# Merged attention in one stage: products of probabilities and values in 32 bit from one copy, exponentials run ahead, VectorE steps reordered

## The reference

```
# branch "b": quantized causal self attention in each block of 128 tokens
q, k, v = bitlinear(x, Wq), bitlinear(x, Wk), bitlinear(x, Wv)   # rope on q, k
p = softmax(causal(q k^T / sqrt(32)));  out = bitlinear(p v, Wo)
x = layernorm(x + out)
# branch "c": gated cross attention to 128 memory tokens
q = rmsnorm(x) wq^T;  k, v = memory wk^T, memory wv^T
p = softmax(masked(q k^T / sqrt(32)));  out = sigmoid(x wg^T) * (p v wo^T)
x = layernorm(x + out)
```

## Time and profile before

| | us |
|---|---|
| time, median of 3 runs | 3196.19 (3192.08 to 3197.03) |
| the profiled execution's own time | 3198.22 |
| span from the first to the last instruction in it | 3196.4 |
| PE busy in the span | 2819.0 (88%) |
| VectorE (DVE) busy | 1944.5 (61%) |
| ScalarE (ACT) busy | 1589.0 (50%) |

### The profile page before, as it was taken

The page is one execution under the profiler, slowest core; times in us unless marked ns, Lnnn a source line. Parts: engine busy times, 40 slices in busy tenths (PEclk is TensorE's granted clock), DMA queues, the critical chain, the costliest instruction groups (busy, mean ns, idle before and its releaser), DMA issues. The chain is left out here.

```text
span 3196.4 us, 50865 instructions
## 1 busy us (share of the span) xinstructions
PE 2819.0 (88%) x17698; PEld 1620.0 (51%) x17698; DVE 1944.5 (61%) x3635; ACT 1589.0 (50%) x3632; POOL 1205.6 (38%) x1234
## 2 busy tenths in 40 slices
PE   6889877999999999699669888887669999999998
PEld 4676653555555555244236555554434444444443
DVE  5788978778788787676567777764442212222224
ACT  7999955655555564643167666654421222122211
POOL 4888967645455452243231111110312221222211
PEclk8999998999999999899879999999779999999999
DMA  4111113000000000400210000000000000000001
GB/s 154 54 42 41 47 51 105 14 8 7 4 7 7 4 3 1 158 1 1 78 41 18 15 13 16 15 15 14 33 31 31 31 31 1 31 31 31 1 1 53
DMA packets 35090, 99.06 MB, mean 31 GB/s; under 512 B 4933, under 2 KB 9413, under 8 KB 31686
## 3 DMA queue, kind: packets, MB, share of 16 engines
q1 hardware_dynamic: 34886, 96.46, 9.1%
HBM read 87.79 MB, written 4.46 MB: 29 GB/s over the span
## 5 line engine op out<-in xcount | busy, mean ns | idle before, releaser
L945 DVE TENSOR_TENSOR m_prod<-m_bank,m_gated 128x512 f32<-128x512 f32 x96 | 66.4, 692 | 507.3 <-ACT m_gated L776 507.3
L720 POOL TENSOR_TENSOR m_aTl<-m_prod,m_aTh 128x512 bf16<-128x512 f32 x96 | 110.9, 1155 | 675.0 <-ACT m_aTh L778 675.0
L1926 POOL TENSOR_TENSOR s_state<-s_state,s_ct 128x512 f32<-128x512 f32 x256 | 326.8, 1307 | 83.1 <-DVE s_state L2101 81.1
L2101 DVE TENSOR_TENSOR_SCAN s_state<-s_decay,s_psd 128x512 f32<-128x512 f32 x256 | 301.9, 1209 | 67.7 <-PE s_psd L2246 34.1
L776 ACT ACTIVATE m_gated<-m_bank 128x512 f32<-128x512 f32 x96 | 57.2, 596 | 549.8 <-PE m_bank L1037 549.8
L1035 PE MATMUL m_bank<-m_xTh,m_wh 128*128 128x512 bf16 x768 | 292.5, 381 | 0.0
L1037 PE MATMUL m_bank<-m_xTh,m_wl 128*128 128x512 bf16 x768 | 292.5, 381 | 0.0
L1036 PE MATMUL m_bank<-m_xTl,m_wh 128*128 128x512 bf16 x768 | 292.5, 381 | 0.0
L2246 PE MATMUL s_psd<-ident,s_v 128*128 128x128 f32 x1024 | 164.7, 286 | 42.4 <-DVE s_state L2101 21.9
L2002 ACT ACTIVATE s_decay<-s_dt,s_nega 128x508 f32<-128x508 f32 x256 | 181.8, 711 | 19.5 <-DVE s_state L2101 19.4
L2015 ACT ACTIVATE s_v<-s_uT,s_bT 128x512 f32<-128x512 f32 x256 | 182.4, 714 | 1.1 <-PE s_psd L2246 1.0
(11 more groups left out here) (499 smaller groups left out, 8142.7 us busy)
## 6 DMA issues: line engine op xcount, KB each, us to landing
m_stage<-in_moe_w_dram SPq DMA_DIRECT2D x8, 2352.0 KB, 9.5
s_ct<-ssm_bc SPq DMA_DIRECT2D x64, 256.0 KB, 3.1
X<-in_x_dram SPq DMA_DIRECT2D x4, 1024.0 KB, 11.6
a_cf<-in_ctxT_dram SPq DMA_DIRECT2D x16, 256.0 KB, 2.6
a_wstage<-in_xa_wq_dram SPq DMA_DIRECT2D x8, 512.0 KB, 3.6
a_wstage<-in_xa_wo_dram SPq DMA_DIRECT2D x8, 512.0 KB, 3.9
f_wstage<-in_ffn_wg_dram SPq DMA_DIRECT2D x4, 1024.0 KB, 6.2
f_wstage<-in_ffn_wu_dram SPq DMA_DIRECT2D x4, 1024.0 KB, 5.2
```

Source lines behind the costliest of these rows:

```text
L1926: pool.tensor_tensor(h, h, ct[t % 4][:, s * P:(s + 1) * P].unsqueeze(1).broadcast_to([P, KB, P]), ALU.mult).then_inc(weighted, 1)
L2101: dve.tensor_tensor_scan(state[i % RING][:, :], decay[t % 2][:, s, :, :].rearrange("p m t -> p (m t)"), ps_d[i % 2][:, :], 0.0, ALU.mult, ...
```

## The change

- The bf16 pairs `pTh`/`pTl` and `vh`/`vl` go. One 32-bit tile `pT` (ScalarE's copy of `ps_t`) and one 32-bit tile `v` take their place, and one 32-bit matmul per head takes the place of three bf16 ones. VectorE's `low_part` (8 in a merged turn) and the rests of both values (one each per turn) go. Where something waited for `low`, it waits for ScalarE's copy (`copied`).
- In sequences that an attention handles alone (`single`: 0 to 3 for `core`, 12 to 15 for `mcore`), odd groups write their probabilities to the other attention's `prob` tile, which is idle there, and ScalarE issues the exponentials of group g+1 ahead of the copy of group g.
- The steps on VectorE and a few on ScalarE stand in another order: steps that release a bank of PE come before layer-norm statistics and divisions.

The core of the diff (the other parts rename semaphores, and remove `values` and `memory_values` from VectorE, with ScalarE's copies writing the 32-bit `v` tiles):

```diff
-        self.vh = [sb(f"{tag}_vh{j}", [P, key_groups * P], BF16, st) for j in range(2)]
-        self.vl = [sb(f"{tag}_vl{j}", [P, key_groups * P], BF16, st) for j in range(2)]
+        self.v = [sb(f"{tag}_v{j}", [P, key_groups * P], F32, st) for j in range(2)]
...
-        self.pTh = sb(f"{tag}_pTh", [P, 4, P], BF16, st)
-        self.pTl = sb(f"{tag}_pTl", [P, 4, P], BF16, st)
+        self.pT = sb(f"{tag}_pT", [P, 4, P], F32, st)
...
+    def alone(self, s):
+
+        return isinstance(s, int) and s in self.single
+
+    def prob_of(self, s, g):
+
+        return self.second if self.alone(s) and g % 2 else self.prob
+
     def turn_probs(self, pe, s, g, other, turned_by_other):
         pe.wait_ge(self.exps.sem, self.exps.at(s, g + 1))
         if g or late(s, 1):
-            pe.wait_ge(self.low.sem, self.low.at(s, g) if g else self.low.at(s - 1))
+            pe.wait_ge(self.copied.sem, self.copied.at(s, g) if g else self.copied.at(s - 1))
         if not isinstance(turned_by_other, int) or turned_by_other:
-            pe.wait_ge(other.low.sem, turned_by_other)
+            pe.wait_ge(other.copied.sem, turned_by_other)
         for h in range(4):
-            mm = pe.transpose(self.ps_t[:, h * P:(h + 1) * P], self.prob[:, h, :], self.fr.ident[:, :])
+            mm = pe.transpose(self.ps_t[:, h * P:(h + 1) * P], self.prob_of(s, g)[:, h, :], self.fr.ident[:, :])
         mm.then_inc(self.turned.sem, 1)
...
             v = (4 * g + h if self.KG == 4 else h) * self.HW
             out = self.ps_v[:, (4 * g + h) * self.HW:(4 * g + h + 1) * self.HW]
-            mm = three(pe, out, (self.pTh[:, h, :], self.pTl[:, h, :]),
-                       (self.vh[p][:, v:v + self.HW], self.vl[p][:, v:v + self.HW]), True, True)
+            mm = pe.matmul(out, self.pT[:, h, :], self.v[p][:, v:v + self.HW], start=True, stop=True)
         mm.then_inc(self.pv.sem, 1)
...
     def exponentials(self, act, s, g, p):
         act.wait_ge(self.shifted.sem, self.shifted.at(s, g + 1))
-        if g or late(s, 1):
+        if self.alone(s):
+            if g >= 2:
+                act.wait_ge(self.turned.sem, self.turned.at(s, g - 1))
+            elif s >= 1:
+                act.wait_ge(self.turned.sem, self.turned.at(s - 1, 3 if g == 0 and self.alone(s - 1) else 4))
+        elif g or late(s, 1):
             act.wait_ge(self.turned.sem, self.turned.at(s, g) if g else self.turned.at(s - 1))
         if g == 0 and late(s, 2):
             act.wait_ge(self.recip.sem, self.recip.at(s - 2))
         for h in range(4):
-            e = act.activation(self.prob[:, h, :], self.ps_s[:, h * P:(h + 1) * P], ACT.Exp,
+            e = act.activation(self.prob_of(s, g)[:, h, :], self.ps_s[:, h * P:(h + 1) * P], ACT.Exp,
                                bias=self.shift[g % 2][:, h:h + 1], scale=self.SCALE,
                                accum_out=self.total[p][:, 4 * g + h:4 * g + h + 1])
         e.then_inc(self.exps.sem, 1)
 
-    def high_part(self, act, s, g):
+    def copy_part(self, act, s, g):
         act.wait_ge(self.turned.sem, self.turned.at(s, g + 1))
         if g or late(s, 1):
             act.wait_ge(self.pv.sem, self.pv.at(s, g) if g else self.pv.at(s - 1))
-        act.activation(self.pTh[:, :, :].rearrange("p h t -> p (h t)"), self.ps_t[:, :], ACT.Copy).then_inc(self.high.sem, 1)
+        act.activation(self.pT[:, :, :].rearrange("p h t -> p (h t)"), self.ps_t[:, :], ACT.Copy).then_inc(self.copied.sem, 1)
...
-    def low_part(self, dve, s, g):
-        dve.wait_ge(self.high.sem, self.high.at(s, g + 1))
-        dve.tensor_tensor(self.pTl[:, :, :].rearrange("p h t -> p (h t)"), self.ps_t[:, :],
-                          self.pTh[:, :, :].rearrange("p h t -> p (h t)"), ALU.subtract).then_inc(self.low.sem, 1)
...
-        core = PairCore(fr, st, "b", 1, PairCore.HW ** -0.5, ps_t, 1)
+        core = PairCore(fr, st, "b", 1, PairCore.HW ** -0.5, ps_t, 1, range(0, LAG))
...
-        mcore = PairCore(fr, st, "c", 4, 1.0, ps_t, 64)
+        mcore = PairCore(fr, st, "c", 4, 1.0, ps_t, 64, range(SEQS - LAG, SEQS))
+        core.second, mcore.second = mcore.prob, core.prob
...
+                    has_b = live(s) and (g < 3 or live(s + 1)) or g == 3 and live(s + 1)
+                    has_c = live(m) and (g < 3 or live(m + 1)) or g == 3 and live(m + 1)
+                    if has_b and core.alone(s):
+                        core.exponentials(act, *following(s, g, p))
...
                     if live(s):
-                        core.high_part(act, s, g)
-                    if live(s) and (g < 3 or live(s + 1)) or g == 3 and live(s + 1):
+                        core.copy_part(act, s, g)
+                    if has_b and not core.alone(s):
                         core.exponentials(act, *following(s, g, p))
+                    if has_c and mcore.alone(m):
+                        mcore.exponentials(act, *following(m, g, p))
                     if g == 0:
                         if live(s + 2):
...
                     if g == 2:
-                        if live(m + 1):
-                            memory_values(m + 1, o)
...
                     if live(m):
-                        mcore.high_part(act, m, g)
-                    if live(m) and (g < 3 or live(m + 1)) or g == 3 and live(m + 1):
+                        mcore.copy_part(act, m, g)
+                    if has_c and not mcore.alone(m):
                         mcore.exponentials(act, *following(m, g, p))
                     if g == 0 and live(m + 1):
                         high(nTh[o][:, :], bank[1][:, :], n_turned, m + 1, n_high)
                     if g == 1 and live(s + 2):
                         qx.scalar(act, s + 2)
-                    if g == 2 and live(m + 2):
-                        context_high(m + 2, p)
+                    if g == 2:
+                        if live(m + 1):
+                            memory_values(m + 1, o)
+                        if live(m + 2):
+                            context_high(m + 2, p)
...
                     if g == 2:
                         if live(s - 1):
                             qo.clip(dve, s - 1)
-                        if live(s - 2):
-                            ln.statistics(dve, s - 2)
                         if live(s + 1):
                             query_low(s + 1, o)
                             key_low(s + 1, o)
                     if g == 3 and live(s - 2):
                         ln.vector_end(dve, s - 2)
-                    if live(s):
-                        core.low_part(dve, s, g)
                     if g == 0:
                         if live(s + 1):
                             rotate_keys(s + 1, o)
-                            values(s + 1, o)
-                        if live(s - 1):
-                            core.divide(dve, s - 1, o)
+                    if g == 2 and live(s - 2):
+                        ln.statistics(dve, s - 2)
                     if g == 3 and live(s + 3):
                         quantize_x(s + 3, o)
 
                     if live(m) and (g < 3 or live(m + 1)) or g == 3 and live(m + 1):
                         mcore.maxima(dve, *following(m, g, p)[:2])
-                    if g == 0 and live(m - 1):
-                        mcore.divide(dve, m - 1, o)
-                    if g == 1:
-                        if live(m - 1):
-                            low(oTl[:, :], bank[1][:, :], oTh[:, :], o_high, m - 1, o_low)
-                        if live(m - 2):
-                            mln.vector_end(dve, m - 2)
+                    if g == 1 and live(m - 1):
+                        low(oTl[:, :], bank[1][:, :], oTh[:, :], o_high, m - 1, o_low)
                     if g == 3:
                         if live(m + 2):
                             norm_mean(m + 2)
                         if live(m - 1):
                             gate_output(m - 1, o)
-                    if live(m):
-                        mcore.low_part(dve, m, g)
-                    if g == 0 and live(m + 1):
-                        low(nTl[o][:, :], bank[1][:, :], nTh[o][:, :], n_high, m + 1, n_low)
-                    if g == 1 and live(m + 1):
-                        queries_low(m + 1, o)
-                    if g == 2 and live(m + 1):
-                        memory_values(m + 1, o)
-                    if g == 3:
-                        if live(m + 2):
-                            norm_apply(m + 2)
+                            memory_end(m - 1)
+                    if g == 0:
+                        if live(s - 1):
+                            core.divide(dve, s - 1, o)
                         if live(m - 1):
-                            memory_end(m - 1)
+                            mcore.divide(dve, m - 1, o)
+                        if live(m + 1):
+                            low(nTl[o][:, :], bank[1][:, :], nTh[o][:, :], n_high, m + 1, n_low)
+                    if g == 1:
+                        if live(m + 1):
+                            queries_low(m + 1, o)
```

(24 more changed lines are left out.)

2 lines of the change are left out of this document (1 added, 1 removed).

## The result

The changed kernel takes 3142.80 us (median of 4 runs, 3140.32 to 3148.05) against 3196.61 us of the kernel before on the same chip: a ratio of 0.9833, 95% interval 0.982 to 0.9845. That is 1.7% faster; 1.2% was predicted (3157 us). The profiled execution took 3140.32 us.

What follows compares the result with a forecast made beforehand. PE nearly sets the pace in merged turns (84% busy), a chain of waits in turns 0 to 2 and 16 to 18. Terms -14 - 1 + 3 - 2 + 0 - 20 - 5 = -39 us gave 3157 us, range 3130 to 3184.

Steps and rivals of the forecast that it cites:

- The 32-bit product: On PE, every group of values: four products take 0.97 us, 0.65 us more than before; 46.8 us over nine merged turns.
- groups of values of about 0.97 us: Sign expected in the changed profile: PE's groups of values take about 0.97 us, against 0.31 us before.
- All four waits should go, 1 us stays: Merged turns: PE's waits for c_pTl, b_ln_r, b_kd, c_qTl (49.6 of 53.7 us) go; 1 us a turn stays for quantized x.
- Nearly the whole gain of the removed waits is given back: Nine merged turns: the 32-bit product's PE time takes back nearly all the removed waits, 335.7 us against 338.1, -2 us.
- Turns 16 to 18: Second attention alone: 22.3 us of waits for exponentials go, PE sets the pace, products add 7.8 us; 78 us, -20.
- Turns 0 to 2: First attention alone: the chain stays but shortens to 21 us a turn, 63 us against 77.4, -14.
- the keys of group 3: Turns 0 to 2: group 3 takes longer, its scores needing new keys and queries that ScalarE splits after the exponentials.
- Half the idle time staying: Rival, merged turns: ScalarE takes VectorE's place and 27 us of PE's idle time stays; 3175 us, chance 0.15.
- Run-ahead worth half: Rival, one-attention turns: VectorE's and ScalarE's other steps are next late, half of 39 us is lost; 3177 us, chance 0.12.
- The dear product: Rival, PE in every group: each product takes four loads, 1.94 us a group; slower, 3262 us, chance 0.08.
- The cheap product: Rival, PE in every group: the product's cost goes with its columns, 0.5 us a group; 3132 us, chance 0.12.
- The wait in front of the transposes of `c_o`: Turns 16 to 18: a new small PE wait, as these transposes need c_nTl from the same bank; 0.9 us a turn.

Runs made afterwards that it cites:

- run with 64 columns: The changed kernel with three of a group's four 32-bit products multiplying 64 columns of the values instead of 32: 3145.21 us, ratio 0.9849.
- run with the early quantization: The changed kernel with ScalarE quantizing x in group 1 ahead of the second attention's copy and exponentials, instead of behind them: 3134.74 us, ratio 0.9809.
- first-attention-only run: The changed kernel with the exponentials' run-ahead kept in the first attention and taken out of the second: 3181.42 us.
- mixed kernel: The changed kernel with bf16 pairs, low parts and rests back in merged turns 4 to 15, 32-bit products kept in one-attention turns: 3126.37 us, ratio 0.9789.

## Why the prediction came out as it did

| stretch | predicted us | measured us |
|---|---|---|
| turns 0 to 2, from the first exponentials | -14 | -10.0 |
| turn 3 | -1 | -0.9 |
| turns 4 and 5 | +3 | -0.1 |
| nine merged turns | -2 | -14.9 |
| turn 15 | 0 | -2.5 |
| turns 16 to 18 | -20 | -23.8 |
| turn 19 | -5 | -3.7 |

The measured column adds up to -55.9 us against -39. In the two profiles the first exponentials also come 3.3 us earlier in the changed kernel, and what follows the last turn takes 1.3 us longer, both in stages that the change doesn't touch. That makes the 57.9 us between the two spans; the medians are 53.8 us apart.

The signs that the prediction named for the changed profile are there: merged turns of 35.9 us (it said 37.3) with PE busy for 97%, turns 16 to 18 of 24.8 us (26), turns 0 to 2 of 21.8 us (21), and 512 pieces for each attention.

*The 32-bit product.* The one clearly mis-sized term. I took 8 x 0.121 = 0.97 us; it is 0.81. The 0.97 was misread: it is the duration that the router's row shows for its eight weight loads, not the time until the next step. The changed kernel shows the same duration for its own eight loads, beside a pace of 0.81 us, and the router's next step starts 0.91 us (2295.50 - 2294.59) after its first piece:

```profile
1907.31 0.97 PEld L2454 LDWEIGHTS b_psv<-b_v,b_pT 128*128 128x128 f32 x8
```
```profile
2295.50 0.66 PE L986 MATMUL m_bank<-ident,m_xs 128*128 128x128 f32 x4
```

So "groups of values of about 0.97 us" came true to the letter (0.98 is shown) while the price is lower. From start to start the router's row gives 0.114 us a piece; why it is 0.10 here is open. Over the 72 groups that is 11.5 of the 12.9 us that the merged turns came out shorter, and over the 24 groups of turns 4, 5 and 15 3.8 of 5.6. The mechanism (two pieces a product, a price that the columns don't set) was right, and the run with 64 columns shows it.

*All four waits should go, 1 us stays.* Right: the four rows are gone, and the one left is 0.9 us a turn, for `b_q_int`, as named. The run with the early quantization shows that it was a real loss.

*"Nearly the whole gain of the removed waits is given back."* Right in sign, too strong. By the runs the order alone takes 28.8 us off the nine turns; the 32-bit product then gives 13.8 back (31.2 us more busy, 17.4 less idle). So half is kept. What I had not seen: the order alone removes half of the idle time (53.7 to 25.6 us) without touching a product. The wait for `b_ln_r` goes and the one for `c_pTl` falls from 24.0 to 6.0 us, while `c_qTl` keeps 7.7 and `b_kd` 4.9 us. What is left is less than the 32-bit product costs, so in merged turns, once the order is changed, the product is a loss.

*Turns 16 to 18.* -20 predicted, -23.8 measured, no wait for `c_prob` over 0.5 us. PE was busy 69.5 us where my terms make 75.6 (70.3 + 7.8 - 2.5); the cheaper product is 1.9 of that, and the clock stood at 1.00 where it had been 0.95. I had the run-ahead pay and the product cost 7.8 us beside it. The runs show that these two don't add: from turn 16 on, the 32-bit product costs 13.5 us without the run-ahead and gives 12.9 with it; the run-ahead gives 9.6 us with bf16 and 36.0 with 32 bit. By the rows above two things tie them together: without the run-ahead the longer product lies in the chain of the exponentials, and with it the low part's way through VectorE's queue holds the chain up. So -20 came close for turns 16 to 18 as a whole; the split into a gain of the run-ahead and a price of the product is not what the runs show.

*Turns 0 to 2.* -14 predicted, -10.0 measured, 21.8 us a turn against 21. PE still waits 11.9 us for `b_prob` and 7.0 for `b_kd`, the keys of group 3 that I had named.

*The rivals.* Half the idle time staying is out (8.2 us are left of 53.7). Run-ahead worth half is out: with 32-bit products it is worth 50 us where I had counted 39. The dear product is out by the 0.81 us. (The Trainium skill's four passes for true FP32, "FP8 and Floating Point Precision", TensorE Precision Notes, would by themselves be an estimated 16 x 0.026 = 0.42 us a group at the pace of bf16 matmuls here; with a full load for each pass I had made 1.94 of them. The trace lies between and shows two pieces; whether each is two passes no run shows.) The cheap product had the right direction: the price lies a third of the way from 0.97 to 0.5. The wait in front of the transposes of `c_o` is there, 2.0 us in three times (I had 0.9 us each), but it is not new: before it was 0.7 us in three times.

What stays open: how much of turns 0 to 2 is the clock. The first-attention-only run has the same instructions there as the change; it took 70.1 us at a granted clock of 0.69, the change 65.5 at 0.81. These are single profiles, so the 4.6 us is an indication only. Some of the 10 us gained there may be the clock's too.

## What to carry to other kernels

Before you replace a split product by a wider type, reorder first and measure what is left: here the wider product removed waits of the merged turns, and a new order removed half of the idle time at no cost to PE. Where one regime is bound by the engine and another by a chain, choose the form for each: the mixed kernel is 16 us below 32 bit everywhere and 26 below bf16 everywhere (14 and 23 by the ratios). And take parts apart in pairs. On top of the order, the 32-bit products alone lose 37 us and the run-ahead alone wins 4, but both together win 14 (34, 7 and 16 by the ratios): each takes out of the chain something in which the other's gain would be lost.

## What the runs showed of the hardware

A 32-bit product of a 128x128 operand is two pieces of 0.10 us each at 32 and at 64 columns, where a bf16 matmul of 32 columns paces at 0.026 us (0.31 us for twelve); so one 32-bit product costs 0.20 us against 0.08 for the three bf16 ones. Products issued twice to one output pace at 0.11 us a piece (0.89 us for eight added ones). The duration that a row of weight loads shows is not their pace: 0.97 us for eight loads whose steps are 0.81 us apart.

The granted clock in turns 0 to 2 differed for the same work: it was 0.68 where PE stood idle 28.5 of 85.8 us (no run-ahead) and 0.81 where it stood idle 17.9 of 65.5 us (the change). The work between the waits was longer at the lower clock, busy 57.3 us in the one and 47.6 in the other. That the shorter waits raised the clock is not shown: the run with the run-ahead in the first attention only had 0.69 there, with PE idle 17.4 of 70.1 us. The two profiles:

```profile
1605.30:1691.10 85.80, 57.28 (x269) 41.30 (x274) 44.64 (x85) 48.60 (x153) 28.52 (x20) 0.68 0.12 37
```
```profile
1600.60:1666.10 65.50, 47.59 (x276) 32.38 (x277) 40.47 (x85) 47.80 (x153) 28.53 (x20) 0.81 0.15 49
```
